# A gated graph network on one core: first states transposed by DMA in two 16-bit planes, and the first units reordered

## The chip, the cores and the metric

The kernel runs on one core of one Trainium2 chip. The metric is the device time of one execution in microseconds (us). Five engines run their own instruction streams and meet at semaphores: TensorE (PE, matmuls; PEld is its weight load), VectorE (DVE), ScalarE (ACT), GpSimd (POOL) and SyncE (SP), which here only issues DMAs. The time before is 384.85 us, the median of three runs (384.82 to 385.16).

## The reference

64 graphs of 128 nodes with 128 features. A layer norm and a ReLU give the first state h; five rounds of a gated update follow, each with its own 128x128 weight; the masked last state is added to x. All weights are float32.

```python
h = jnp.maximum(_layernorm(x, axis=-1), 0.0)
A = (adj != 0).astype(x.dtype)
for l in range(5):
    m = jnp.einsum('bnd,de->bne', h, weight[l])
    agg = jnp.einsum('bij,bid->bjd', A, m)
    gi = agg @ w_ih.T + b_ih
    gh = h @ w_hh.T + b_hh
    r = sigmoid(i_r + h_r)
    z = sigmoid(i_z + h_z)
    n = tanh(i_n + r * h_n)
    h = (1.0 - z) * n + z * h
out = x + h * nodemask[..., None]
```

## The kernel before

**Tiles and units.** Four graphs make a tile: 128 partitions by 512 columns. There are 16 tiles, in three groups (tiles 0 to 3, 4 to 9, 10 to 15). A unit is one layer of one tile, numbered K = 0 to 79: within a group all tiles do layer 0, then all do layer 1, and so on. A tile of the first group comes back every 4 units, one of the others every 6. Weight products of the input side are folded once per layer into `v_hi`/`v_lo` (`fold`, L321); `u_hi`/`u_lo` belong to the state side.

**Two layouts.** Every float32 value is split into two float16 parts, so a product is three matmuls (L250 to L252). `nat` holds a state with nodes on the partitions, for the aggregation (L308, L309: `ps_s<-a,nat`, 8 matmuls a unit). `hp` holds it with features on the partitions, for the gates (`ps_r`, `ps_z`, `ps_hn`, `ps_in`). `h` is the float32 state, features on the partitions. After a new state, ACT makes its high part, POOL its low part (L703), and a DMA transpose on SP's queue brings both from `hp` to `nat` (`transpose`, L203) for the tile's next layer.

**The first state of a tile.** DVE takes the moments (L494, L503), POOL the reciprocal root (L674, L676), DVE the shift (`shift_of`, L515), ACT the normalised values `h0` with nodes on the partitions (L375) and their high part in `nat` (L383), POOL the low part (L680). SP transposes `nat` to `hp` by DMA (`transpose_first` of SP, L197). The float32 `h` comes another way: PE transposes `h0` with four matmuls against an identity into the PSUM bank `ps_t` (L317), and ACT copies that to `h` (`transposed`, L395). For tile 0 also `hp` comes from `ps_t`.

**The order.** It is written out per engine. PE's unit K is: nine state products (`h_products`), six products of r and z with s (`s_product`), the aggregation of unit K + 1, three products for n. DVE's unit is: `r_times_hn` (L531), `n_input` (L537), `s_low` (L525) of unit K + 1, at most one preparation step, then the new state (L543, L548). The preparation of tiles 4 to 15 is spread over units by `prep` (L50 to L53): `prep[t]` is the unit of stage 0, each stage one unit later. Stage 0 moments, 1 aggregate and root, 2 shift and adjacency (POOL L686, 1.94 us each), 3 and 4 the two halves of the layer norm, 5 high and low part and PE's transposes, 6 the DMA transpose and ACT's copy to `h`. Tiles 4 to 9 have `prep` 1, 4, 7, 10, 13, 16, so that stage 2 of a tile stands in the same unit as stage 5 of the tile ahead. Within PE's loop the transposes stand ahead of the aggregation of the next unit.

**The start and the end.** Before unit 0 PE runs blank matmuls (`awake`, L325) while the inputs and weights arrive, and a power-of-two scale is taken from bounds on the weights (`weight_scale`, `scale_from_bound`). The last unit has its own code (`masked_open`, L557; `last_result`, L565).

The names above with these lines are what the change touches.

Of the kernel before, what the change touches and what calls it, by code (L numbers as in the profile page):

```python
# [32 lines left out]
def gnn_kernel(nc, x, xT, adj, mask_row, fold_lhs, w_ihT, w_hhT, bias_ih, bias_hh, ident, out):  # L33
# [35 lines left out]
    with ExitStack() as ctx:  # L69
# [42 lines left out]
        rstd = sb("rstd", [P, 2, TG])  # L112
        shift = sb("shift", [P, 2, TG])
# [5 lines left out]
        nat = ctx.enter_context(nc.sbuf_tensor("nat", [P, RING, 2 * TG, P], F16))  # L119

# [15 lines left out]
        ends_loaded = [sem(f"ends_loaded{i}") for i in range(FRING)]  # L136
        stored = [sem(f"stored{i}") for i in range(FRING)]
# [9 lines left out]
        bn_done, aggr_done, var_done, rstd_done = sem("bn_done"), sem("aggr_done"), sem("var_done"), sem("rstd_done")  # L147
        shift_done, h0_done, a_done, t_mm = sem("shift_done"), sem("h0_done"), sem("a_done"), sem("t_mm")
        nat_hi_init, nat_lo_init = sem("nat_hi_init"), sem("nat_lo_init")
        h_hi_init, h_lo_init, h_init = sem("h_hi_init"), sem("h_lo_init"), sem("h_init")  # L150
# [6 lines left out]
        last_masked, last_h_masked, last_kept, open_done, last_out, last_hn_mm = sem("last_masked"), sem("last_h_masked"), sem("last_kept"), sem("open_done"), sem("last_out"), sem("last_hn_mm")  # L157
# [27 lines left out]
        def _(sp):  # L185
# [33 lines left out]
            load_x(0)  # L219
            sp.dma_start(fold_in[:].rearrange("p (l d) -> p l d", l=L), fold_lhs).then_inc(fold_loaded, 16)  # L220
# [10 lines left out]
            for K in range(1, N + 2):  # L231
# [16 lines left out]
        def _(pe):  # L248
# [81 lines left out]
            def first():  # L330
                pe.wait_ge(blank_set, 1)
                awake(18)
# [6 lines left out]
                awake(8)  # L339
                pe.wait_ge(top_done, 1)  # L340
                pe.wait_ge(u_lo_done, 1)

            first()
            for K in range(N):
                h_products(K)
                if K == N - 1:
                    break
                if K == 0:
                    aggregate(0)
                    transpose_first(1)  # L350
# [17 lines left out]
        def _(act):  # L368
            def layernorm(t, half):
                act.wait_ge(shift_done, t + 1)  # L370
                if t >= LN:
                    act.wait_ge(nat_lo_init, t - LN + 1)
                    act.wait_ge(t_mm, t - LN + 1)
# [22 lines left out]

            def s_high(K):
# [15 lines left out]
            def gate_n(K):  # L413
                act.wait_ge(npre_done, K + 1)
                n = ps_in[K % 2] if K < N - 1 else r
                nc.scalar.activation(n[:], ps_in[K % 2][:], ACT.Tanh, bias=b_ih[:, 2:3],  # L416
# [6 lines left out]

            def v_high(l):
                act.wait_ge(v_mm, l + 1)
                nc.scalar.activation(v_hi[:, l], ps_f[:, 0:CG], ACT.Copy, scale=scale[:, 0:1]).then_inc(v_hi_done, 1)

# [5 lines left out]
            def first():  # L433
                act.dma_start(whh_sb[:], w_hhT).then_inc(whh_loaded, 16)
                act.dma_start(wih_sb[:], w_ihT).then_inc(wih_loaded, 16)

# [5 lines left out]
                act.wait_ge(whh_loaded, 16)  # L442
                act.wait_ge(scale_done, 1)
                nc.scalar.activation(u_hi[:], whh_sb[:], ACT.Copy, scale=scale[:, 0:1]).then_inc(u_hi_done, 1)
                natural_high(0)
                transposed(0)
                layernorm(1, 0)
                layernorm(1, 1)
                v_high(0)
                s_high(0)  # L450
                natural_high(1)
                if DIRECT > 1:
                    transposed_high(1)
# [3 lines left out]
            for K in range(N):  # L457
# [337 lines left out]
```

## Time and profile before

| | before |
|---|---|
| median of three runs | 384.85 us |
| profiled execution, whole | 386.38 us |
| its span | 384.4 us |
| PE busy | 367.2 us, 96% |
| DVE, ACT, POOL busy | 308.0, 295.0, 273.8 us (80%, 77%, 71%) |
| DMA transposes, hp to nat and nat to hp | 64 and 15 |
| granted TensorE clock, mean | 0.989 |

The span runs from the first to the last instruction of the profiled execution; its whole time is 1.98 us longer. A busy share is over the whole span: an engine with 80% can be at its limit in one stage and idle in another. Where instructions overlap in the pipeline, a row's duration is longer than the distance from its start to the next one's; it is the distance that an engine's order has to pay.

### The profile page before, as it was taken

How to read it: one execution, taken by the hardware profiler on the slowest of the kernel's cores; microseconds unless marked ns; L12 is line 12 of the kernel's file. 1: busy time of each engine (PE TensorE's matmuls, PEld its weight loads, DVE VectorE, ACT ScalarE, POOL GpSimd, SP SyncE). 2: the span in 40 equal slices, each digit the busy share in tenths (PEclk: the TensorE clock that was granted, in tenths of full speed). 3: DMA queues.
4: the chain of work that ended last, by engine and by line, in shares of the span. 5: the costliest groups of instructions: out<-in, count | busy, mean ns of one | idle time of the engine just before them, and what ended most of it. 6: DMA issues, size and time to landing. Idle time of an engine off the chain costs nothing.

```text
span 384.4 us, 6567 instructions
## 1 busy us (share of the span) xinstructions
PE 367.2 (96%) x2182; PEld 188.7 (49%) x2182; DVE 308.0 (80%) x568; ACT 295.0 (77%) x489; POOL 273.8 (71%) x245
## 2 busy tenths in 40 slices
PE   5867999999999999999999999999999999999992
PEld 2433555555555555555555555555545555555541
DVE  5676788888887778888888898877777778777776
ACT  3587789889978777888898977788776777677662
POOL 4456677887897678777769595947876655544796
PEclk9899999999999999999999999999999999999997
DMA  8733346396573645444366664306633342298422
GB/s 239 171 55 82 84 114 125 66 210 112 131 180 82 97 96 113 107 113 82 83 90 148 98 151 121 107 10 158 136 84 84 88 77 56 57 183 214 97 82 82
DMA packets 107793, 42.89 MB, mean 112 GB/s; under 512 B 84833, under 2 KB 101473, under 8 KB 107761
## 3 DMA queue, kind: packets, MB, share of 16 engines
q1 hardware_dynamic: 107232, 41.76, 49.5%
q10 hardware_dynamic: 432, 0.66, 0.6%
q8 instruction: 17, 0.28, 0.3%
q14 instruction: 16, 0.12, 0.1%
q0 software_dynamic: 96, 0.07, 0.1%
HBM read 17.57 MB, written 4.19 MB: 57 GB/s over the span
## 4 chain that ended last, share of the span: by engine, by line
PE 89%; DVE 4%; DMA 3%; ACT 1%; issue 1%; POOL 1%; DVEq 0%; POOLq 0%
PE ps_r L250 9%; PE ps_r L251 9%; PE ps_z L251 9%; PE ps_z L252 9%; PE ps_r L252 9%; PE ps_z L250 9%; PE ps_s L309 4%; PE ps_s L308 4%; PE ps_in L252 4%; PE ps_hn L251 4%; PE ps_in L251 4%; PE ps_hn L250 4%; PE ps_in L250 4%; PE ps_hn L252 4%; PE ps_t L317 2%; DMA hp<-nat 2%
## 5 line engine op out<-in xcount | busy, mean ns | idle before, releaser
L698 POOL TENSOR_TENSOR zh<-z,h 128x512 f32<-128x512 f32 x80 | 101.5, 1269 | 85.8 <-ACT z L411 85.4
L405 ACT ACTIVATE r<-ps_r,b_sum,unscale 128x512 f32<-128x512 f32 x80 | 62.2, 777 | 56.7 <-PE ps_r L252 54.9
L531 DVE SCALAR_TENSOR_TENSOR rhn<-ps_hn,b_hn,r 128x512 f32<-128x512 f32 x80 | 60.0, 750 | 26.2 <-ACT r L405 26.1
L703 POOL TENSOR_TENSOR hp<-h,hp 128x512 f16<-128x512 f32 x64 | 74.0, 1156 | 0.0
L537 DVE TENSOR_TENSOR ps_in<-ps_in,rhn 128x512 f32<-128x512 f32 x80 | 55.9, 699 | 19.6 <-PE ps_in L252 18.3
L416 ACT ACTIVATE ps_in<-ps_in,b_ih,unscale 128x512 f32<-128x512 f32 x79 | 59.2, 750 | 13.1 <-DVE ps_in L537 11.2
L543 DVE SCALAR_TENSOR_TENSOR ps_in<-z,ps_in 128x512 f32<-128x512 f32 x79 | 54.6, 691 | 10.4 <-ACT ps_in L416 10.4
L411 ACT ACTIVATE z<-ps_z,b_sum,unscale 128x512 f32<-128x512 f32 x80 | 61.5, 769 | 0.7 <-PE ps_z L252 0.7
L548 DVE TENSOR_TENSOR h<-zh,ps_in 128x512 f32<-128x512 f32 x78 | 53.6, 687 | 8.7 <-POOL zh L698 0.8
L525 DVE TENSOR_TENSOR s_lo<-ps_s,s_hi 128x512 f16<-128x512 f32 x80 | 54.4, 680 | 1.4 <-ACT s_hi L399 1.4
L399 ACT CAST s_hi<-ps_s 128x512 f16<-128x512 f32 x80 | 46.6, 583 | 2.6 <-PE ps_s L309 1.4
L308 PE MATMUL ps_s<-a,nat 128*128 128x128 f16 x320 | 44.3, 219 | 0.0
L309 PE MATMUL ps_s<-a,nat 128*128 128x128 f16 x320 | 44.3, 219 | 0.0
L422 ACT CAST hp<-h 128x512 f16<-128x512 f32 x64 | 40.5, 633 | 0.0
L308 PEld LDWEIGHTS ps_s<-a,nat 128*128 128x128 f16 x320 | 31.3, 98 | 8.3 <-POOL nat L680 0.6
L309 PEld LDWEIGHTS ps_s<-a,nat 128*128 128x128 f16 x320 | 31.3, 98 | 7.8
L250 PE MATMUL ps_r<-hp,u_hi 128*128 128x512 f16 x80 | 30.4, 379 | 5.0 <-DMA hp<-nat 5.0
L375 ACT ACTIVATE h<-x_in,shift,rstd 128x128 f32<-128x128 f32 x64 | 27.6, 482 | 6.9 <-DVE shift L515 6.9
L250 PE MATMUL ps_r<-s_hi,v_hi 128*128 128x512 f16 x80 | 30.3, 379 | 1.0 <-DVE s_lo L525 1.0
L250 PE MATMUL ps_z<-s_hi,v_hi 128*128 128x512 f16 x80 | 30.3, 379 | 0.0
L251 PE MATMUL ps_r<-hp,u_hi 128*128 128x512 f16 x80 | 30.3, 379 | 0.0
L252 PE MATMUL ps_r<-hp,u_lo 128*128 128x512 f16 x80 | 30.3, 379 | 0.0
(88 smaller groups left out, 745.9 us busy)
## 6 DMA issues: line engine op xcount, KB each, us to landing
x_in<-in_x SPq DMA_DIRECT2D x16, 256.0 KB, 4.6
adj_in<-in_adj SPq DMA_DIRECT2D x16, 256.0 KB, 4.1
x_out<-in_xT SPq DMA_DIRECT2D x16, 256.0 KB, 3.2
mask_in<-in_mask_row SPq DMA_DIRECT2D x16, 256.0 KB, 3.9
out<-x_out SPq DMA_DIRECT2D x15, 256.0 KB, 2.3
nat<-hp SPq DMA_TRANSPOSE x64, 3.1
fold_in<-in_fold_lhs SPq DMA_DIRECT2D x1, 320.0 KB, 4.8
out<-x_out ACTq DMA_DIRECT2D x1, 256.0 KB, 2.3
```

The lines of the kernel that those rows point to most:

```text
L250: nc.tensor.matmul(ps[:], w_hi, m_hi, start=start, stop=False)
L251: nc.tensor.matmul(ps[:], w_hi, m_lo, start=False, stop=False)
L252: return nc.tensor.matmul(ps[:], w_lo, m_hi, start=False, stop=stop)
L308: nc.tensor.matmul(block_of(ps_s, q), block_of(nat_hi(t), q), a_q, start=True, stop=False)
L309: last = nc.tensor.matmul(block_of(ps_s, q), block_of(nat_lo(t), q), a_q, start=False, stop=True)
L405: nc.scalar.activation(r[:], ps_r[:], ACT.Sigmoid, bias=b_sum[:, 0:1], scale=unscale[:, 0:1]).then_inc(r_done, 1)
L411: nc.scalar.activation(z[:, K % 2], ps_z[:], ACT.Sigmoid, bias=b_sum[:, 1:2], scale=unscale[:, 0:1]).then_inc(z_done, 1)
L416: nc.scalar.activation(n[:], ps_in[K % 2][:], ACT.Tanh, bias=b_ih[:, 2:3], scale=unscale[:, 0:1]).then_inc(n_done, 1)
L531: nc.vector.scalar_tensor_tensor(out=rhn[:], in0=ps_hn[:], scalar=b_hn[:, 0:1], in1=r[:], op0=ALU.add, op1=ALU.mult).then_inc(rhn_done, 1)
L537: nc.vector.tensor_tensor(ps_in[K % 2][:], ps_in[K % 2][:], rhn[:], ALU.add).then_inc(npre_done, 1)
L698: nc.gpsimd.tensor_tensor(zh[:, K % 2], z[:, K % 2], h[:, t % RING], ALU.mult).then_inc(zh_done, 1)
L703: nc.gpsimd.tensor_tensor(h_lo(t), h[:, t % RING], h_hi(t), ALU.subtract).then_inc(h_lo_done, 1)
```

## The change

Tiles 4 to 15 no longer use PE for `h`. At stage 6 ACT copies `h0` to `halves` as 16-bit words, all low words first and then all high words (`split`); SP transposes those 256 KB by one more DMA, right behind the `nat` to `hp` one (`transpose_halves`); at stage 8 DVE interleaves the two planes into `h` (`join`, an integer copy). The sequences of PE and ACT lose 12 groups of four transposes and 12 copies from `ps_t`. The shift is now a product on POOL, from a negated mean that DVE writes right behind the aggregate (`minus_mean`). Tiles 10 to 15 are prepared every 5 units in place of every 4.

At the start the two gate weight loads go from ACT's queue to SP's; 24 and 4 blank matmuls stand where 18 and 8 stood; unit 0's state products are ordered by which operand comes first; `natural_high(1)` stands ahead of `v_high(0)` on ACT, and the layer norm of tile 2 ahead of unit 0's gates; PE's transposes of tile 1 stand behind unit 0's products of r and z. In the last unit ACT copies the mask row to PSUM, and n stays in PSUM.

```diff
-        gap = 3 if t < starts[1] + GROUPS[1] else 4
+        gap = 3 if t < starts[1] + GROUPS[1] else 5
...
+            def transpose_halves(t):
+                sp.wait_ge(split_done, t - FIRST + 1)
+                if t - FIRST >= 2:
+                    sp.wait_ge(h_init, t - 1)
+                sp.dma_start_transpose(halves_t[:, t % 2], halves[:, t % 2].rearrange("p b c -> p (b c)")).then_inc(
+                    halves_loaded[t % 2], 16)
...
                 if K in tile_at_stage[6]:
                     transpose_first(tile_at_stage[6][K])
+                    transpose_halves(tile_at_stage[6][K])
...
-                if 2 <= K + 1 < FIRST:
+                if K + 1 < FIRST:
                     transpose_first(K + 1)
-                if K in tile_at_stage[5]:
-                    transpose_first(tile_at_stage[5][K])
...
+            def split(t):
+                act.wait_ge(h0_done, 2 * t + 2)
+                if t - FIRST >= 2:
+                    act.wait_ge(halves_loaded[t % 2], 16 * ((t - FIRST) // 2))
+                nc.scalar.copy(halves[:, t % 2], h0[:, t % LN].bitcast(U16).rearrange("p (c b) -> p b c", b=2)).then_inc(
+                    split_done, 1)
...
                 if K in tile_at_stage[6]:
-                    transposed(tile_at_stage[6][K])
+                    split(tile_at_stage[6][K])
...
+                nc.vector.tensor_scalar(minus_mean[:, t % 2], mean_var[:, t % 2, :, 0], -1.0, None,
+                                        ALU.mult).then_inc(minus_done, 1)
...
+            def join(t):
+                dve.wait_ge(halves_loaded[t % 2], 16 * ((t - FIRST) // 2 + 1))
+                if t >= RING:
+                    dve.wait_ge(masked, t - RING + 1)
+                nc.vector.tensor_copy(h[:, t % RING].bitcast(U16).rearrange("p (c b) -> p b c", b=2),
+                               halves_t[:, t % 2].rearrange("p (b g) c -> p b (g c)", b=2)).then_inc(h_init, 1)
...
-                if K in tile_at_stage[2]:
-                    shift_of(tile_at_stage[2][K])
+                if K in tile_at_stage[8]:
+                    join(tile_at_stage[8][K])
...
+                pool.wait_ge(minus_done, t + 1)
+                pool.wait_ge(rstd_done, t + 1)
+                nc.gpsimd.tensor_tensor(shift[:, t % 2], minus_mean[:, t % 2], rstd[:, t % 2], ALU.mult).then_inc(shift_done, 1)
...
-                n = ps_in[K % 2] if K < N - 1 else r
...
+                nc.scalar.copy(ps_s[:], mask_in[:, f]).then_inc(mask_moved, 1)
...
-                nc.vector.scalar_tensor_tensor(out=ps_s[:], in0=z[:, K % 2], scalar=1.0, in1=mask_in[:, f],
+                dve.wait_ge(mask_moved, 1)
+                nc.vector.scalar_tensor_tensor(out=mask_in[:, f], in0=z[:, K % 2], scalar=1.0, in1=ps_s[:],
                                                op0=ALU.subtract, op1=ALU.mult).then_inc(open_done, 1)
```

The order of ACT's first instructions, before: four layer-norm pieces (`h<-x_in,shift,rstd`) per tile, `nat<-h` the high part of `natural_high`.

```order
L387 ACTIVATE hp<-ps_t 128x512
L444 ACTIVATE u_hi<-whh_sb,scale 128x384
L383 ACTIVATE nat<-h 128x512
L395 ACTIVATE h<-ps_t 128x512
L375 ACTIVATE h<-x_in,shift,rstd 128x128 x4
L426 ACTIVATE v_hi<-ps_f,scale 128x384
L399 CAST s_hi<-ps_s 128x512
L383 ACTIVATE nat<-h 128x512
L405 ACTIVATE r<-ps_r,b_sum,unscale 128x512
```

The same stretch of ACT in the changed kernel:

```order
L416 ACTIVATE hp<-ps_t 128x512
L463 ACTIVATE u_hi<-whh_sb,scale 128x384
L412 ACTIVATE nat<-h 128x512
L404 ACTIVATE h<-x_in,shift,rstd 128x128 x4
L412 ACTIVATE nat<-h 128x512
L467 ACTIVATE v_hi<-ps_f,scale 128x384
L436 CAST s_hi<-ps_s 128x512
L424 ACTIVATE h<-ps_t 128x512
L404 ACTIVATE h<-x_in,shift,rstd 128x128 x4
L442 ACTIVATE r<-ps_r,b_sum,unscale 128x512
```

The high part of tile 1 moved ahead of `v_hi` and `s_hi`, the copy of tile 0 from `ps_t` behind them, and the layer norm of tile 2 ahead of the first `r`.

SP's queue in units 10 and 11, before (`nat<-hp` is `transpose` of the unit just done, `hp<-nat` the first transpose of tile 5):

```order
L194 DMA adj_in<-in_adj 128x4x128
L189 DMA x_in<-in_x 128x4x128
L201 DMA_TRANSPOSE hp<-nat 128x8x128
L206 DMA_TRANSPOSE nat<-hp 128x8x128
L212 DMA x_out<-in_xT 128x512
L213 DMA mask_in<-in_mask_row 128x512
```

The same place in the changed kernel:

```order
L202 DMA adj_in<-in_adj 128x4x128
L197 DMA x_in<-in_x 128x4x128
L209 DMA_TRANSPOSE hp<-nat 128x8x128
L215 DMA_TRANSPOSE halves_t<-halves 128x8x128
L221 DMA_TRANSPOSE nat<-hp 128x8x128
L227 DMA x_out<-in_xT 128x512
L228 DMA mask_in<-in_mask_row 128x512
```

One more DMA transpose stands ahead of the one that unit 10's state leaves by.

DVE in units 11 and 12, before (`shift` belongs to tile 7):

```order
L503 BN_AGGR mean_var<-bn 128x2 x4
L543 SCALAR_TENSOR_TENSOR ps_in<-z,ps_in 128x512
L548 TENSOR_TENSOR h<-zh,ps_in 128x512
L531 SCALAR_TENSOR_TENSOR rhn<-ps_hn,b_hn,r 128x512
L537 TENSOR_TENSOR ps_in<-ps_in,rhn 128x512
L525 TENSOR_TENSOR s_lo<-ps_s,s_hi 128x512
L515 SCALAR_TENSOR_TENSOR shift<-mean_var,rstd 128x4
L543 SCALAR_TENSOR_TENSOR ps_in<-z,ps_in 128x512
```

The same place in the changed kernel (`COPY h<-halves_t` is `join` of tile 5):

```order
L548 BN_AGGR mean_var<-bn 128x2 x4
L551 TENSOR_SCALAR minus_mean<-mean_var 128x4
L583 SCALAR_TENSOR_TENSOR ps_in<-z,ps_in 128x512
L588 TENSOR_TENSOR h<-zh,ps_in 128x512
L571 SCALAR_TENSOR_TENSOR rhn<-ps_hn,b_hn,r 128x512
L577 TENSOR_TENSOR ps_in<-ps_in,rhn 128x512
L565 TENSOR_TENSOR s_lo<-ps_s,s_hi 128x512
L620 COPY h<-halves_t 128x2x512
L583 SCALAR_TENSOR_TENSOR ps_in<-z,ps_in 128x512
```

The join stands where the shift stood, and a small instruction came in behind the aggregate.

## Rows read from the trace of the kernel before

**Rows 1.** Windows: us, busy PE PEld DVE ACT POOL, PEclk, DMA share, GB/s.

```profile
75.00:95.00 20.00, 20.00 (x119) 10.44 (x118) 17.57 (x38) 18.19 (x33) 15.66 (x15) 1.00 0.74 151
...
270.00:370.00 100.00, 100.00 (x602) 50.92 (x600) 79.05 (x116) 72.17 (x113) 66.27 (x56) 1.00 0.48 105
```

**Rows 2.** Waits of PE: waiting line, releaser, us in total, times, longest.

```profile
PE ps_r L250 <- DMA hp<-nat: 5.0, 3, 2.1
```

**Rows 3.** Timeline of the start, all engines: start, us, instruction.

```profile
11.93 0.58 ACT L395 ACTIVATE h<-ps_t 128x512 f32<-128x512 f32 x1
...
12.17 1.11 DVE L515 SCALAR_TENSOR_TENSOR shift<-mean_var,rstd 128x4 f32<-128x4 f32 x1
...
13.32 1.65 ACT L375 ACTIVATE h<-x_in,shift,rstd 128x128 f32<-128x128 f32 x4 [0.81 <-DVE shift L515]
...
15.17 1.01 POOL L676 TENSOR_TENSOR rstd<-var_eps,neg_half 128x4 f32<-128x4 f32 x1
...
18.05 1.16 POOL L680 TENSOR_TENSOR nat<-h,nat 128x512 f16<-128x512 f32 x1 [1.87 <-ACT nat L383]
18.08 1.41 DVE L508 TENSOR_SCALAR a<-adj_in 128x512 f16<-128x512 f32 x1
...
22.42 0.39 PE L250 MATMUL ps_r<-hp,u_hi 128*128 128x512 f16 x1 [1.57 <-DMA hp<-nat]
...
36.59 0.39 PE L250 MATMUL ps_r<-hp,u_hi 128*128 128x512 f16 x1 [1.28 <-DMA hp<-nat]
```

**Rows 4.** Window just ahead of unit 0.

```profile
11.00:14.20 3.20, 3.20 (x9) 1.21 (x8) 3.16 (x8) 2.39 (x7) 1.17 (x1) 0.52 1.21 290
```

**Rows 5.** Timeline of PE, units 8 to 10.

```profile
59.34 0.38 PE L250 MATMUL ps_r<-hp,u_hi 128*128 128x512 f16 x1
...
63.67 0.38 PE L250 MATMUL ps_r<-hp,u_hi 128*128 128x512 f16 x1
...
68.44 0.38 PE L250 MATMUL ps_r<-hp,u_hi 128*128 128x512 f16 x1
...
70.38 0.38 PE L250 MATMUL ps_r<-s_hi,v_hi 128*128 128x512 f16 x1
```

**Rows 6.** Instructions of the tiles shift, a and ps_t: ns min/median/max.

```profile
L515 DVE SCALAR_TENSOR_TENSOR shift<-mean_var,rstd x16: 148/690/1112, 7.8 to 244.0; 128x4 f32<-128x4 f32 x16
...
L508 DVE TENSOR_SCALAR a<-adj_in x4: 394/414/1405, 13.2 to 28.6; 128x512 f16<-128x512 f32 x4
...
L395 ACT ACTIVATE h<-ps_t x16: 577/586/594, 11.9 to 262.0; 128x512 f32<-128x512 f32 x16
```

**Rows 7.** Timeline of unit 9, DVE and POOL.

```profile
69.25 0.68 DVE L525 TENSOR_TENSOR s_lo<-ps_s,s_hi 128x512 f16<-128x512 f32 x1
...
69.84 0.55 DVE L515 SCALAR_TENSOR_TENSOR shift<-mean_var,rstd 128x4 f32<-128x4 f32 x1
...
70.34 1.94 POOL L686 TENSOR_SCALAR a<-adj_in 128x512 f16<-128x512 f32 x1
```

**Rows 8.** Timeline of units 10 to 13, SP, DVE, POOL and PE.

```profile
78.25 2.00 SPq L201 DMA_TRANSPOSE hp<-nat  x1
...
80.30 1.43 SPq L206 DMA_TRANSPOSE nat<-hp  x1
...
83.92 0.55 DVE L515 SCALAR_TENSOR_TENSOR shift<-mean_var,rstd 128x4 f32<-128x4 f32 x1
...
84.42 1.93 POOL L686 TENSOR_SCALAR a<-adj_in 128x512 f16<-128x512 f32 x1
...
85.75 0.22 PE L308 MATMUL ps_s<-a,nat 128*128 128x128 f16 x1
```

**Rows 9.** DMA issues between 78.2 and 81.2 us: us from issue to landing.

```profile
hp<-nat SPq DMA_TRANSPOSE x1, 4.5
nat<-hp SPq DMA_TRANSPOSE x1, 3.4
```

**Rows 10.** Timeline of the end.

```profile
378.36 1.57 DVE L562 SCALAR_TENSOR_TENSOR ps_s<-z,mask_in 128x512 f32<-128x512 f32 x1
378.48 0.78 ACT L416 ACTIVATE r<-ps_in,b_ih,unscale 128x512 f32<-128x512 f32 x1 [1.66 <-DVE ps_in L537]
```

More of the change, by code:

```diff
@@ L112, in gnn_kernel @@
         rstd = sb("rstd", [P, 2, TG])
+        minus_mean = sb("minus_mean", [P, 2, TG])
         shift = sb("shift", [P, 2, TG])
@@ L136, in gnn_kernel @@
         ends_loaded = [sem(f"ends_loaded{i}") for i in range(FRING)]
+        halves_loaded = [sem(f"halves_loaded{i}") for i in range(2)]
         stored = [sem(f"stored{i}") for i in range(FRING)]
@@ L256, in h_product, with first_h_products @@
                 return three(ps, block_of(u_hi, k), block_of(u_lo, k), h_hi(t), h_lo(t), True, k == 2)
+            def first_h_products():
+                banks = (ps_r, ps_z, ps_hn)
+                pe.wait_ge(h_hi_init, 1)
+                pe.wait_ge(u_hi_done, 1)
+                for k, ps in enumerate(banks):
+                    nc.tensor.matmul(ps[:], block_of(u_hi, k), h_hi(0), start=True, stop=False)
+                pe.wait_ge(h_lo_init, 1)
+                for k, ps in enumerate(banks):
+                    nc.tensor.matmul(ps[:], block_of(u_hi, k), h_lo(0), start=False, stop=False)
+                pe.wait_ge(u_lo_done, 1)
+                for k, ps in enumerate(banks):
+                    nc.tensor.matmul(ps[:], block_of(u_lo, k), h_hi(0), start=False, stop=k == 2)
             def h_products(K):
                 t, l = units[K]
-                if l == 0 and t < DIRECT:
-                    pe.wait_ge(h_lo_init, t + 1)
-                elif l == 0:
+                if l == 0:
                     pe.wait_ge(hp_loaded[t % RING], 16 * (t // RING + (t % RING >= DIRECT)))
@@ L338, in first @@
                 fold(0)
-                awake(8)
+                awake(4)
                 pe.wait_ge(top_done, 1)
-                pe.wait_ge(u_lo_done, 1)
             first()
             for K in range(N):
-                h_products(K)
+                if K:
+                    h_products(K)
+                else:
+                    first_h_products()
                 if K == N - 1:
@@ L414, in gate_n @@
                 act.wait_ge(npre_done, K + 1)
-                n = ps_in[K % 2] if K < N - 1 else r
-                nc.scalar.activation(n[:], ps_in[K % 2][:], ACT.Tanh, bias=b_ih[:, 2:3],
+                nc.scalar.activation(ps_in[K % 2][:], ps_in[K % 2][:], ACT.Tanh, bias=b_ih[:, 2:3],
                                      scale=unscale[:, 0:1]).then_inc(n_done, 1)
@@ L422, in state_high, with u_high @@
                 nc.scalar.copy(h_hi(t), h[:, t % RING]).then_inc(h_hi_done, 1)
+            def u_high():
+                act.wait_ge(whh_loaded, 16)
+                act.wait_ge(scale_done, 1)
+                nc.scalar.activation(u_hi[:], whh_sb[:], ACT.Copy, scale=scale[:, 0:1]).then_inc(u_hi_done, 1)
             def v_high(l):
@@ L508, in first_adjacency @@
                 nc.vector.tensor_scalar(a[:, t], adj_in[:, t], 0.0, None, ALU.not_equal).then_inc(a_done, 1)
-            def shift_of(t):
-                dve.wait_ge(rstd_done, t + 1)
-                if t >= 2:
-                    dve.wait_ge(h0_done, 2 * (t - 1))
-                nc.vector.scalar_tensor_tensor(out=shift[:, t % 2], in0=mean_var[:, t % 2, :, 0], scalar=-1.0,
-                                               in1=rstd[:, t % 2], op0=ALU.mult, op1=ALU.mult).then_inc(shift_done, 1)
             def transposed_low(t):
```

63 lines of the change are left out of this document (32 added, 31 removed).

## The prediction

> **What bounds the kernel now.** I read the windows first, then PE's waits, then the timelines of the start, of units 8 to 13 and of the end. Between 270 and 370 us PE is busy for all 100.00 us at a granted clock of 1.00, and it is just as full between 75 and 95 us, where DVE has 2.43 us of 20 idle and ACT 1.81 [rows 1]. PE waits within its unit loop three times for the first transpose of a tile, 5.0 us in all [rows 2], and the last of these ends at 36.59 us [rows 3]. So there are three stretches. Up to 36.59 us the chain through each tile's first state decides (layer norm, high part, low part, DMA transpose). From there to some 377 us it is PE's instruction count, and nothing else. At the end it is the chain of the last unit. An instruction taken from PE in the middle is worth its full length, as long as DVE, ACT, POOL and the DMAs still arrive in time; the question of this change is whether they do.
>
> **The start.** Unit 1 began at 22.42 when its transpose had landed; that was issued when POOL's low part ended at 18.05 + 1.16, and POOL had waited 1.87 us for ACT's high part [rows 3]. Its own work, the root of tile 2, ended at 15.17 + 1.01 = 16.18. In the change ACT doesn't copy `ps_t` at 11.93 but starts tile 1's layer norm there (before: 13.32, after a wait for DVE's shift, which took 1.11 us for four elements), needs 1.65 us for it and some 0.6 for the high part: ready at 14.2. So POOL's root becomes what comes last. It carries the shift as well, which I take at 0.2 us, but DVE gets to the aggregate of tile 2 up to 1.0 us earlier, without that shift. The low part starts at 15.4 to 16.4 in place of 18.05: 1.7 to 2.6 us gained for unit 1. For unit 2 the whole layer norm now lies ahead of the first gates, where half of it, 0.8 us, used to come behind n; that adds up to 0.9. For unit 3 the rest of its chain is the same, with the shift found ready. I take 3.3 us at the start of unit 3, between 2.0 and 4.2. PE's own work could hold this back: between 11.0 and 14.2 us the granted clock was 0.52 [rows 4], the lower level of 1.2 GHz, after PE had stood idle with short breaks of work. If the first unit falls into such a stretch, its nine state products take twice as long, some 1.9 us more; that delays s, and I expect it to cost the sum 1 us of the 3.3, not all, since POOL's chain doesn't pass through it. Moving the weight loads behind the first x on SP adds two issues ahead of fold and tile 1, a shift of 1 us that I cost at nothing: the order of the bytes that the weight bound needs is still x, weights, fold.
>
> **Twelve groups of transposes leave PE.** From unit 8 to unit 9 PE needs 63.67 - 59.34 = 4.33 us, from 9 to 10, with a group of four transposes, 68.44 - 63.67 = 4.77 [rows 5]. That is 0.44 us for each group, 12 x 0.44 = 5.3 us, all in the part where PE is full. ACT loses 12 copies of 0.586 us [rows 6] and gets 12 copies of 1024 16-bit words. Nothing shows such a copy; between 0.59 (the same bytes) and 1.17 (twice the elements) I take 1.0. That is 0.4 us more once in three units of 13 us, of which ACT has 9% idle, 1.2 us: it fits, though the gate behind it can be 0.4 us late.
>
> **What DVE pays.** The join moves 1024 16-bit words from SBUF to SBUF. A copy of 512 elements takes 0.414 undisturbed [rows 6], the subtraction of 512 elements 0.68 [rows 7]: below 0.41 is excluded, twice 0.68 = 1.36 is the upper end, and I take 0.75, near the copy, whose form it has. But that copy has a maximum of 1.405, and the row with 1.41 began at 18.08 beside POOL's subtraction, which ended at 19.21 [rows 3, 6]; the copy ran its 0.4 us, roughly, behind it. The shift, 148 ns at least, has a median of 690, and in unit 9 it ends at 70.39 just as POOL goes over to the adjacency at 70.34 [rows 6, 7]. So these DVE forms wait for a running POOL instruction, and the join, in the shift's place, will wait 0.5 us too: 1.2 in place of 0.55. `minus_mean` costs between 0.15 and, if it also waits for POOL, 0.7; I take 0.4. In units 9 to 17 there are three such rounds of three units. Each adds 0.65 + 0.4 to DVE and takes 0.44 from PE's time, 1.5 us, against an idle share of 2.43/20 x 13.4 = 1.6. The margin of PE itself is small: `s_lo` ends at 69.93, and PE takes it at 70.38 [rows 5, 7], 0.45 us. It fits almost exactly; I book 0.5 us of stalls, bounds 0 and 2.5 (join 1.36 and `minus_mean` 0.7 in all three rounds, less the margin). For tiles 10 to 15 a round has five units and the join's unit has no other preparation on DVE: free. Shift on POOL: 0.2 us, twelve times, where POOL has 20% idle: free.
>
> **What the DMA queue pays.** The added transpose stands between two others on SP. In unit 10 the `hp` one was issued at 78.25 and took the queue 2.00 us, and unit 10's own went out at 80.30, behind it [rows 8]. It landed 3.4 us later [rows 9], at 83.7, and PE's aggregation of that tile came at 85.75 [rows 8]: 2.05 us of margin. The change takes 0.44 of it (one group of transposes fewer between) and puts the new issue ahead, 1.3 to 2.0 us. That leaves between +0.3 and -0.4, and up to 1.1 less if it lands after 4.5, as `hp` did [rows 9]. The same holds in units 7 and 13; later tiles come back after six units and have 8.7 us more. What waits on SP behind it are only loads for later. I book 0.3 us each, 1.0 in all, bounds 0 and 4.
>
> The Trainium skill (VectorE: DVE Perf Modes, The three transpose paths) gives 390 ns for a 128x128 bf16 transpose on TensorE and 1309 ns by DMA, and advises TensorE where PSUM will do. By that the eight blocks of the planes would take 10.5 us, an estimate from that page, and each join would come six or seven us late. The trace disagrees: eight blocks land in 3.4 to 4.5 us.
>
> **A missed boundary.** The new planes go out at 80.3 and land between 83.7 and 84.8 by the two landings. The join of tile 5 comes up where the shift did, at 83.92, or 0.44 earlier. POOL goes over to the adjacency at 84.42 [rows 8]. If the planes are there, the join slips in ahead of it; if not, it waits for the planes and then for 1.93 us of adjacency. That can happen in units 9, 12, 15 and 18. A miss costs about 1.9 us less the margin of 0.45, some 1.5. I book 0.7, half a miss.
>
> The Trainium skill (SBUF — State Buffer, SBUF: two separate sides) states it as a lock on a port pair: whichever of GpSimd and a two-port DVE instruction starts first keeps it for its whole length. By that a missed boundary costs the whole adjacency, as booked; the waits of the shift above agree with it.
>
> **The end.** The masked product started at 378.36 and took 1.57 us, to 379.93, beside POOL, while n was ready at 378.48 + 0.78 = 379.26 [rows 10]. With the mask in PSUM it has one SBUF input less and should take 0.7, to 379.06, so n decides: 0.7 us gained. The copy to PSUM fits on ACT between r and n.
>
> **Sum.** Against the profiled execution's span of 384.4: -3.3 (start) - 5.3 (transposes) - 0.7 (end) + 0.5 + 1.0 + 0.7 (DVE, queue, boundary) = -7.1, so 377.3. The span and what lies around it make 386.38, but the median of the runs, 384.85, is 0.45 above the span; the predicted median is 377.75.
>
> **Rivals.** (a) *The full gain.* No stall in the middle: the bookings of 2.2 us fall away, and a start at its bound of 4.2: 377.75 - 2.2 = 375.6, at best 374.7. For it speaks that no part of units 4 to 79 shows a PE wait today. Chance 0.22. (b) *Boundaries missed.* Join late in three or four of units 9, 12, 15, 18: 3 x 1.5 or 4 x 1.5 in place of 0.7, and the queue at 2: 377.75 + 3.8 to 6.3 = 381.5 to 384. For it: the landing of 83.7 to 84.8 against 84.42. Against: the first of the four has hardly any loads beside it, and a stall of PE moves the next join later, into its landing. Chance 0.13. (c) *Slower: a slow interleave.* The write skips every second 16-bit word. If the join takes more than the upper end of the rows, it costs all 12 tiles. DVE's chain in a unit leaves 1.2 us between `s_lo` and the new state before PE stalls, so with a join of J the stall is 12 x (J + 0.2 - 1.2), and the gain of 9.3 is gone at J = 1.8. At J = 2.2 it would be 14.4: 384.85 - 9.3 + 14.4 = 390. No row shows a DVE instruction with more than 1.36 us per 1024 elements undisturbed. Chance 0.03. (d) *The reorder brings nothing*, because the loads or the clock take it back: start 0.5 in place of 3.3: 380.6. Chance 0.07.
>
> My forecast has 0.55. The range holds it with (a) nearly whole, (d) and the near part of (b): 375.0 to 381.8. Two tenths of a percent, 0.8 us, is about what a measurement of this kernel can tell. Faster holds for the forecast, (a), (d) and most of (b): 0.95; slower for (c) and the far end of (b), 0.03; the same 0.02.
>
> **What would show it.** PE's first matmul of unit 3 near 33.3 us. Units of 4.33 us without exception from unit 18 on. The join near 0.75 us at its shortest and 1.2 in the middle. PE waits in units 10 to 18 of some 2 us, on `s_lo` or on `nat`, and none later. DVE's last three instructions without a gap behind n. Wrong would be: PE waits above 4 us after unit 3, a join above 1.4 us alone, or a first unit 3 later than 35 us.

## The result, and the profile after

The changed kernel takes 383.44 us (median of seven runs, 381.68 to 383.97) against 384.82 (seven runs, 384.72 to 386.43): a ratio of 0.9946, interval 0.9927 to 0.9964. It is faster, by 0.5% in place of the 1.8% of the forecast, and outside the forecast's range. Its profiled execution took 383.44 us, with a span of 381.6: PE 96% busy, DVE 83%, ACT 78%, POOL 74%.

To see where the time went I use one measure throughout: the distance from PE's first matmul of a unit to that of the next. It is 4.33 us for a unit that waits for nothing, 4.77 with a group of four transposes [rows 5]. What a unit has over 4.33 is its stall (four units of the first group also hold a fold of 0.65 us, in every kernel here; unit 78 has 0.70 over in all of them, which is left out). Every stretch of the two profiles, predicted and measured, in us:

| | predicted | measured |
|---|---|---|
| start of unit 3 | 3.3 earlier | 2.7 earlier (36.59 to 33.91) |
| twelve groups of transposes | -5.3 | -5.3 |
| stalls, units 3 to 77 | +2.2 | +5.6, in 21 units |
| end of the span after unit 79 starts | -0.7 | -0.4 (10.73 to 10.30) |
| span | 384.4 to 377.3 | 384.4 to 381.6 |
| from span to median | +0.45 | +1.84 |

The 36.59 us and the last row belong together: the first profile of the kernel before was of a long execution. In its second profile, below, unit 3 starts at 35.26, so that the start gained 1.35 us and not 2.7; what the first row shows too much comes back in the last.

Windows of the changed kernel, columns as in [rows 1]:

```profile
75.00:95.00 20.00, 19.73 (x113) 9.35 (x111) 18.53 (x39) 18.17 (x33) 17.47 (x18) 1.00 0.86 180
270.00:370.00 100.00, 100.00 (x606) 50.94 (x604) 79.47 (x118) 72.14 (x114) 66.60 (x56) 1.00 0.47 106
```

The late stretch is unchanged. Between 75 and 95 us DVE has 1.5 us idle in place of 2.4, POOL 2.5 in place of 4.3. The waits of PE and of its weight loads, and DVE's for the planes (columns as in [rows 2]):

```profile
PEld ps_r L268 <- DVE s_lo L565: 11.7, 21, 1.9
...
PE ps_r L268 <- DMA hp<-nat: 3.0, 2, 2.1
PE ps_r L268 <- DVE s_lo L565: 2.8, 4, 1.7
...
PEld ps_s L338 <- DMA nat<-hp: 1.6, 3, 0.6
DVE h L620 <- DMA halves_t<-halves: 1.2, 3, 0.5
```

Against [rows 2], 5.0 us of waiting for a tile's first transpose have become 3.0, and a new wait for `s_lo` is there: 21 times. (A weight load that waits costs less than its wait, since it normally runs ahead.)

The start, timeline (all engines), answering to [rows 3]:

```profile
11.34 0.20 POOL L719 TENSOR_TENSOR shift<-minus_mean,rstd 128x4 f32<-128x4 f32 x1
11.80 1.64 ACT L404 ACTIVATE h<-x_in,shift,rstd 128x128 f32<-128x128 f32 x4
...
13.47 0.63 ACT L412 ACTIVATE nat<-h 128x512 f16<-128x512 f32 x1
...
15.21 0.20 POOL L719 TENSOR_TENSOR shift<-minus_mean,rstd 128x4 f32<-128x4 f32 x1
15.36 1.16 POOL L723 TENSOR_TENSOR nat<-h,nat 128x512 f16<-128x512 f32 x1
...
19.73 0.39 PE L268 MATMUL ps_r<-hp,u_hi 128*128 128x512 f16 x1 [0.86 <-DMA hp<-nat]
...
26.80 0.39 PE L268 MATMUL ps_r<-hp,u_hi 128*128 128x512 f16 x1 [2.12 <-DMA hp<-nat]
```

ACT's layer norm of tile 1 starts at 11.80 (predicted 11.93), the high part is ready at 14.10 (14.2), POOL's low part starts at 15.36 (15.4 to 16.4), and the shift on POOL takes its 0.2 us. The chain of tile 1 went as worked out. But behind the 2.12 us wait the clock fell (windows of the changed kernel):

```profile
26.00:28.00 2.00, 1.20 (x5) 0.54 (x6) 1.90 (x8) 1.97 (x5) 0.00 (x0) 0.85 0.04 6
28.00:30.00 2.00, 2.00 (x6) 0.68 (x5) 0.50 (x1) 0.53 (x2) 1.88 (x2) 0.50 0.00 0
30.00:32.00 2.00, 2.00 (x10) 1.00 (x9) 0.00 (x0) 0.72 (x2) 0.39 (x1) 0.80 0.75 141
```

0.50 is the lower level of 1.2 GHz. Unit 3 came at 33.91, 7.11 us after unit 2.

In the middle, the tile of the planes (ns min/median/max):

```profile
L215 SPq DMA_TRANSPOSE halves_t<-halves x12: 1231/1356/2507, 63.4 to 264.6; - x12
L620 DVE COPY h<-halves_t x12: 746/1366/1843, 66.8 to 267.9; 128x1024 uint16<-128x1024 uint16 x12
its engine sat idle before it (us, times) until:
  DMA halves_t<-halves: 1.2, 3
...
DMA to landing us min/median/max: 3.1/3.4/4.2
```

The join needs 0.746 us at its shortest, as I took it, but 1.37 in the median and 1.84 at most. One of the costliest, timeline of DVE, POOL and PE, in unit 24 and the two behind it:

```profile
135.49 1.26 POOL L757 TENSOR_TENSOR x_out<-x_out,mask_in 128x512 f32<-128x512 f32 x1
135.75 1.60 DVE L620 COPY h<-halves_t 128x1024 uint16<-128x1024 uint16 x1
...
136.71 1.75 POOL L741 TENSOR_TENSOR zh<-z,h 128x512 f32<-128x512 f32 x1
...
138.49 0.69 DVE L588 TENSOR_TENSOR h<-zh,ps_in 128x512 f32<-128x512 f32 x1 [0.55 <-POOL zh L741]
...
140.55 0.68 DVE L565 TENSOR_TENSOR s_lo<-ps_s,s_hi 128x512 f16<-128x512 f32 x1
...
141.29 0.39 PE L268 MATMUL ps_r<-s_hi,v_hi 128*128 128x512 f16 x1 [0.57 <-DVE s_lo L565]
```

The join is issued 0.26 us after a POOL product starts and does most of its 0.75 us of work behind that product's end (136.75). It ends at 137.35, 0.60 us behind that end; in this profile 11 of the 12 joins end 0.59 to 0.61 us behind the POOL instruction with two SBUF inputs that was running when they were issued. Then POOL's next product, `zh`, takes 1.75 in place of 1.27, because the join runs. DVE waits 0.55 for `zh`, and everything behind moves: `s_lo` is late, PE stands still. A join thus costs twice, once by its own wait and once by the delay that it passes on. Not all of this stall is the join's: unit 26 has 0.96 us here, and 0.34 in the run below in which PE does the transposes again.

The end, DVE's and ACT's part, answering to [rows 10]:

```profile
375.99 0.68 DVE L603 SCALAR_TENSOR_TENSOR mask_in<-z,ps_s 128x512 f32<-128x512 f32 x1
376.12 0.75 ACT L452 ACTIVATE ps_in<-ps_in,b_ih,unscale 128x512 f32<-128x512 f32 x1 [1.17 <-DVE ps_in L577]
376.90 0.70 DVE L611 TENSOR_TENSOR ps_in<-mask_in,ps_in 128x512 f32<-128x512 f32 x1 [0.23 <-ACT ps_in L452]
377.63 0.69 DVE L614 TENSOR_TENSOR x_out<-x_out,ps_in 128x512 f32<-128x512 f32 x1
```

The masked product takes 0.68 in place of 1.57 and n decides, as predicted. Counted from the start of unit 79, DVE's last instruction ends 0.8 us earlier than before; but the store behind it landed after 2.6 us and not after 2.3, and the span gained 0.4.

### The profile page after: what moved, and what is told of

Read it like the earlier page. It is cut to its first block, busy times and chain, and to the rows that moved or that the text cites. A ratio compares the mean times of both kernels' runs of the same rounds, so it can differ in the third digit from the quotient of the medians.

```text
span 381.6 us, 6527 instructions
## 1 busy us (share of the span) xinstructions
PE 366.9 (96%) x2136; PEld 181.8 (48%) x2136; DVE 317.8 (83%) x580; ACT 298.9 (78%) x490; POOL 280.8 (74%) x261
## 4 chain that ended last, share of the span: by engine, by line
PE 70%; DVE 13%; POOL 4%; DMA 3%; issue 3%; ACT 3%; SPq 2%; DVEq 0%; POOLq 0%; ACTq 0%
PE ps_r L268 7%; PE ps_z L269 7%; PE ps_z L268 7%; PE ps_z L270 7%; PE ps_r L269 7%; PE ps_r L270 7%; PE ps_s L339 4%; PE ps_s L338 4%; PE ps_in L270 4%; PE ps_in L269 4%; PE ps_in L268 4%; PE ps_hn L269 3%; PE ps_hn L270 3%; PE ps_hn L268 3%; DVE ps_in L577 2%
## 5 line engine op out<-in xcount | busy, mean ns | idle before, releaser
L741 POOL TENSOR_TENSOR zh<-z,h 128x512 f32<-128x512 f32 x80 | 102.7, 1284 | 79.5 <-ACT z L448 79.2
L452 ACT ACTIVATE ps_in<-ps_in,b_ih,unscale 128x512 f32<-128x512 f32 x80 | 60.1, 751 | 21.6 <-DVE ps_in L577 20.1
L268 PE MATMUL ps_r<-hp,u_hi 128*128 128x512 f16 x79 | 30.0, 379 | 3.4 <-DMA hp<-nat 3.0
L269 PE MATMUL ps_r<-s_lo,v_hi 128*128 128x512 f16 x80 | 30.5, 381 | 0.0
L270 PE MATMUL ps_r<-s_hi,v_lo 128*128 128x512 f16 x80 | 30.3, 379 | 0.0
```

What stands on the lines that cost most here:

```text
L268: nc.tensor.matmul(ps[:], w_hi, m_hi, start=start, stop=False)
L269: nc.tensor.matmul(ps[:], w_hi, m_lo, start=False, stop=False)
L270: return nc.tensor.matmul(ps[:], w_lo, m_hi, start=False, stop=stop)
L452: nc.scalar.activation(ps_in[K % 2][:], ps_in[K % 2][:], ACT.Tanh, bias=b_ih[:, 2:3], scale=unscale[:, 0:1]).then_inc(n_done, 1)
L741: nc.gpsimd.tensor_tensor(zh[:, K % 2], z[:, K % 2], h[:, t % RING], ALU.mult).then_inc(zh_done, 1)
```

## The experiments

Each was timed against the kernel before, whose median was 384.8 to 384.9 in every comparison.

**The kernel before, once more** (no edit).

> The kernel before, unchanged, for a second profile. Its first profile took 386.38 us while its runs have a median of 384.8, so 1.5 us of that span are not usual. Theory: they lie ahead of unit 3 (first matmul of unit 3 near 35.1 us in place of 36.59), and then the reordered start gained 1.2 us in the median and not the 2.7 us that the two profiles show. Rival: unit 3 starts at 36.6 again, and the 1.5 us lie elsewhere.

385.06 us, span 383.1. From its timeline:

```profile
16.66 1.16 POOL L680 TENSOR_TENSOR nat<-h,nat 128x512 f16<-128x512 f32 x1 [0.33 <-ACT nat L383]
...
21.03 0.39 PE L250 MATMUL ps_r<-hp,u_hi 128*128 128x512 f16 x1 [1.57 <-DMA hp<-nat]
...
35.26 0.39 PE L250 MATMUL ps_r<-hp,u_hi 128*128 128x512 f16 x1
```

There the clock was 1.00 from 10 to 28 us, unit 3 started at 35.26 and not at 36.59, and all behind it took the same time. So the profile of [rows 3, 4] was that of a long execution (386.38 us against a median of 384.85). What differs between the two is the stretch at 0.52: there the first matmul of unit 0 came at 14.27, here at 12.73, and ACT's high part of tile 1, which stands behind the `s_hi` of unit 0, followed it. POOL waits 0.33 us for that high part here, and 1.87 in [rows 3]. The usual start of POOL's low part, against which the changed kernel's 15.36 has to be held, is 16.66 and not 18.05.

The 0.45 of my sum is no error of its own, since the forecast is the median before less 7.1 us whatever the span. The error lies in the start, which I read from the long execution. In every profiled execution from here on the time is 1.8 to 2.0 us above the span.

**Transposes back on PE; start, end, shift on POOL and the gap of 5 kept.**

```diff
-                    split(tile_at_stage[6][K])
+                    transposed(tile_at_stage[6][K])
...
-                    transpose_halves(tile_at_stage[6][K])
...
-                    join(tile_at_stage[8][K])
...
+                    transpose_first(tile_at_stage[5][K])
```

> The changed kernel with the transposes of tiles 4 to 15 back on PE and ACT's copy from ps_t; no split, no third DMA, no join; start, end, shift on POOL and the gap of 5 stay. Theory (the joins' stalls eat what the transposes free): the middle has 5.3 us of transposes again and nearly no waits, so 383.4 +- 0.6 us, as the changed kernel. Rival (2 us or more of the stalls come from the negated mean on DVE and the shift on POOL): these waits stay, 385 us or more.

382.38 us, ratio 0.9942 (0.9928 to 0.9956): within the intervals the same as the whole change, and 0.4 below the range that I expected. What gained is the start and the end; the DMA transposes with their joins bring nothing net. The twelve units with transposes take 4.77 each, so the 5.3 us are real and are all given back. Unit 3 starts at 32.44 here, without a stretch at the lower clock: the start is worth 2.8 us against 35.26. Two stalls of 0.34 and 0.20 in units 26 and 29 are there without any join.

**The planes are made and moved, but the interleave isn't done.** `h` of tiles 4 to 15 gets zeros (512 columns for tiles 4 to 9, one for 10 to 15).

```diff
-                nc.vector.tensor_copy(h[:, t % RING].bitcast(U16)...
+                columns = TILE if t < GROUPS[0] + GROUPS[1] else 1
+                nc.vector.memset(h[:, t % RING, 0:columns], 0.0).then_inc(h_init, 1)
```

> The changed kernel with the interleave left out: tiles 4 to 9 get a plain DVE memset of the same 512 float32 columns, tiles 10 to 15 a memset of one column, so the state of these tiles is wrong and only the time counts. Split and the third DMA stay. Theory (DVE's join on the shared port is what PE waits for): the waits of units 30 to 56 vanish (1.9 us) and those before shrink to what DMA and ACT leave: 379.5 to 380.5. Rival (SP's queue and ACT's split): not under 382.5.

379.65 us (378.17 to 380.33), ratio 0.9856 (0.9839 to 0.9874). With split, DMA and queue all kept, the median is 3.8 us below the changed kernel's. The profiled execution is the fastest of its four: unit 3 starts at 32.01, the clock holds, and its stalls add up to 2.1 us, those of the changed kernel to 5.6. The difference of 3.5 is what the join costs beyond the memset in its place, which takes 0.48 us for each of tiles 4 to 9 and 0.06 for the others; it is one profile against one. One stall of 0.60 (unit 16, `nat` late) is the queue's.

**Tiles 4 to 9 by PE, 10 to 15 by DMA.**

```diff
+HALF = 10
...
-                    split(tile_at_stage[6][K])
+                    (split if tile_at_stage[6][K] >= HALF else transposed)(tile_at_stage[6][K])
...
-                if K in tile_at_stage[8]:
+                if tile_at_stage[8].get(K, 0) >= HALF:
```

> Tiles 4 to 9 transposed by PE as before, tiles 10 to 15 by DMA in two planes. Theory: PE has 2.6 us more of transposes, and the waits of units 10 to 26 (3.5 us) are nearly gone, those of units 30 to 56 (1.9 us) stay: 382.5, range 381.8 to 383.3. Rival (waits in units 10 to 26 come from the shift and the negated mean): 385.

381.32 us, ratio 0.9915 (0.9899 to 0.9931), 0.5 below the range expected. So even half of the change is better than the whole. The joins of tiles 10 to 15, which I had called free, leave stalls of 0.13, 0.22, 0.21, 0.21 and 0.48 us in units 31, 36, 41, 46 and 51, 1.25 in all, for 2.6 us of transposes removed.

**The changed kernel, once more** (no edit).

> The changed kernel again, beside the others. In its first profile TensorE's granted clock was 0.50 from 28 to 30 us, in unit 2, after PE had waited 2.1 us for a transpose; unit 3 began at 33.91. In the three profiles with the same start that had no such stretch it began at 32.0 to 32.5. Theory (a clock stretch of 1.5 us comes in some executions): runs fall into two clusters about 1.5 us apart, near 381.8 and 383.4. Rival (the spread has another cause): a profile with unit 3 near 32.5 still takes 383.4.

383.15 us (381.72 to 384.44), ratio 0.9957 (0.9939 to 0.9974). The clock fell in the same place (0.50 between 28 and 30 us), unit 3 at 34.08. The two clusters of runs did not come: the six lie at 381.72, 382.62, 383.00, 383.29, 384.01 and 384.44. The stalls added up to 6.1 us in the profiled execution: units 15 and 17 had 0.49 and 0.62 where the first profile had 0.31 and 0.30. Ahead of unit 17 one join missed its place: the planes of tile 6 came 0.35 us late, and the adjacency had begun 0.08 us before the join (DVE and POOL):

```profile
95.78 1.94 POOL L729 TENSOR_SCALAR a<-adj_in 128x512 f16<-128x512 f32 x1
95.86 1.13 DVE L620 COPY h<-halves_t 128x1024 uint16<-128x1024 uint16 x1 [0.35 <-DMA halves_t<-halves]
```

The join took 1.13 us. It did not wait for the adjacency's end at 97.72.

**Transposes on PE, and tiles 10 to 15 every 4 units again.**

```diff
-        gap = 3 if t < starts[1] + GROUPS[1] else 5
+        gap = 3 if t < starts[1] + GROUPS[1] else 4
```

> The transposes of tiles 4 to 15 on PE and the gap of 4 again: only the start, the end, the shift on POOL and the negated mean remain of the change. With the gap of 5 PE stalled 0.34 us in unit 26 and 0.20 in unit 29 beyond its transposes. Theory (the gap of 5 puts the adjacency of tile 10 into unit 23, where POOL already has the final of tile 2): both stalls go, 0.5 us less, 381.8. Rival (they come from the shift on POOL): unchanged, 382.4.

382.97 us, ratio 0.9948 (0.9933 to 0.9964); the 0.5 us less than the run before it can't be seen in the times. In the profile the stall of 0.34 in unit 26 is gone, so the gap of 5 made it: it puts tile 10's adjacency into unit 23, beside POOL's results of finished tiles. The one in unit 29 (0.23) stays. Three runs are at 381.9 to 382.3 and three at 383.6 to 383.7, with mean clocks of 0.996 to 0.998 and 0.992 to 0.993. The distance is about the 1.5 us that the stretch at 0.50 costs in the start, but no profile of a slower one shows where its time went.

**Tiles 10 to 15 by DMA, with the join behind the new state and not ahead of it** (the edit against the kernel with tiles 4 to 9 by PE).

```diff
-                if tile_at_stage[8].get(K, 0) >= HALF:
-                    join(tile_at_stage[8][K])
...
+                if tile_at_stage[8].get(K, 0) >= HALF:
+                    join(tile_at_stage[8][K])
                 if K == N - 2:
                     masked_state(K)
```

> Tiles 10 to 15 by DMA, tiles 4 to 9 by PE, as in the run before it, but the join stands behind the new state of its unit, when POOL has nothing to do. Theory (what hurts is the wait for a running POOL instruction, 1.57 us in place of 0.75): the join takes 0.75, the waits of units 31 to 56 (1.25 us) go, 380.1. Rival (the DVE time itself hurts, or the delayed POOL instruction): no gain or a loss, 381.3 or more.

379.93 us (379.35 to 380.14), ratio 0.9870 (0.9857 to 0.9882). The join's row in this kernel (ns min/median/max):

```profile
L624 DVE COPY h<-halves_t x6: 741/746/1074, 158.1 to 266.4; 128x1024 uint16<-128x1024 uint16 x6
```

And one of them in the timeline of POOL and DVE:

```profile
177.82 1.16 POOL L750 TENSOR_TENSOR hp<-h,hp 128x512 f16<-128x512 f32 x1
...
179.73 0.74 DVE L624 COPY h<-halves_t 128x1024 uint16<-128x1024 uint16 x1
...
180.92 1.27 POOL L745 TENSOR_TENSOR zh<-z,h 128x512 f32<-128x512 f32 x1 [1.94 <-ACT z L452]
```

In the changed kernel the join of this tile was issued at 180.10 with POOL's low part running from 179.91, and took 1.57. One place further down DVE's order, POOL stands idle and waits for z. The five stalls of 1.25 us are gone.

**All joins behind the new state** (tiles 4 to 8 one unit later), the negated mean on POOL, tile 10 one unit later.

```diff
+    joining = {prep[t] + (9 if t < 9 else 8): t for t in prep}
+    prep[10] += 1
...
+                nc.gpsimd.tensor_tensor(minus_mean[:, t % 2], mean_var[:, t % 2, :, 0], minus_one[:], ALU.mult).then_inc(minus_done, 1)
```

> All of tiles 4 to 15 by DMA, the join behind the new state (tiles 4 to 8 one unit later than in the change, the others in the same unit), the negated mean on POOL in place of DVE, and the preparation of tile 10 one unit later. Theory (DVE's waits for the port and POOL's crowding in unit 23 are what the freed 5.3 us went into): the waits of PE fall from 5.7 to 1.5 us or less, 379.0, range 378.0 to 380.5. Rival (SP's queue and ACT's longer copy are as dear as the port): 382 or more.

381.08 us (380.52 to 382.45), ratio 0.9910 (0.9896 to 0.9923): 2.4 us better than the changed kernel, 2.1 worse than expected. About 1 us of that lies in the start: the clock was 0.81 and 0.53 between 14 and 20 us, unit 3 starts at 33.82 where the late join of tiles 10 to 15 alone had 32.88, and the mean clock of all six runs is 0.986 to 0.992. The median join is at 0.74 here too, but a stall of 0.86 us is left in unit 26:

```profile
133.77 1.27 POOL L758 TENSOR_TENSOR x_out<-x_out,mask_in 128x512 f32<-128x512 f32 x1
...
135.00 1.27 POOL L742 TENSOR_TENSOR zh<-z,h 128x512 f32<-128x512 f32 x1
...
136.30 0.69 DVE L588 TENSOR_TENSOR h<-zh,ps_in 128x512 f32<-128x512 f32 x1 [1.09 <-POOL zh L742]
136.90 1.08 DVE L620 COPY h<-halves_t 128x1024 uint16<-128x1024 uint16 x1
...
137.88 0.73 DVE L571 SCALAR_TENSOR_TENSOR rhn<-ps_hn,b_hn,r 128x512 f32<-128x512 f32 x1
...
140.06 0.39 PE L271 MATMUL ps_r<-s_hi,v_hi 128*128 128x512 f16 x1 [0.57 <-DVE s_lo L565]
```

Two things add up. POOL's own order is full around unit 24, which delays `zh` and the new state without any join. And tile 9's join, now behind that late state, takes 1.08 beside POOL's low part and stands ahead of `rhn` and `s_lo`. The run before this one has no join there: its new state came no earlier (136.53), `rhn` followed at once, and its stall in unit 26 is 0.33. So a place behind the new state is free only while DVE has time there. Unit 13 has 0.71, 0.5 of it a wait for `nat`.

**The changed kernel with 14 more blank matmuls** (6 ahead of the first product of s, 8 behind unit 1), to keep PE busy in the start.

```diff
+                    awake(6)
...
+                if K == 1:
+                    awake(8, ps_f)
```

> The changed kernel with 14 more blank matmuls: 6 ahead of unit 0's products with s and 8 ahead of unit 2, where PE otherwise waits 1.7 and 2.1 us. Theory (the spread of 381.7 to 384.4 us is a stretch at half clock after one of these waits): no granted clock under 1.00 between 14 and 36 us, unit 3 near 32.5, the runs close together, median 381.8. Rival (the spread comes from the middle): the clock is full, but the runs still spread over 2 us.

384.44 us (twelve runs, 382.74 to 384.76), ratio 0.9976 (0.9964 to 0.9988). The clock was 1.00 all through the start, and unit 3 came 0.7 us earlier, at 33.17. Yet the kernel is slower than the changed one and its runs still spread over 2 us, as the rival said; my theory that the spread of the runs is the clock's alone fell. The stalls come to 7.6 us, and 2.07 of them are in unit 20. The tile of the planes between 104 and 112 us:

```profile
L623 DVE COPY h<-halves_t x1: 854/854/854, 110.7 to 110.7; 128x1024 uint16<-128x1024 uint16 x1
its engine sat idle before it (us, times) until:
  DMA halves_t<-halves: 2.2, 1
...
DMA to landing us min/median/max: 5.3/5.3/5.3
```

Issued at 105.39, like the changed kernel's at 105.41, these planes landed after 5.3 us and not after 3.5. The join had to wait 2.20 us in DVE's order, and PE lost 2.07. That is the late join of rival (b) in one tile; which transfer delayed the planes stays open.

**Tiles 10 to 15 by DMA with the late join, and other units for their preparation**: 26, 30, 35, 39, 42 and 46, away from POOL's full units; then the same with the blank matmuls.

```diff
+    prep.update({10: 26, 11: 30, 12: 35, 13: 39, 14: 42, 15: 46})
```

> As the hybrid with the late join, and tiles 10 to 15 prepared from units 26, 30, 35, 39, 42, 46, so that tile 10's adjacency stays clear of the finals of tiles 0 to 3 and no join meets a moments step. Theory: the waits of units 26 and 29 (0.55 us) go, nothing new comes: 379.4. Rival (a shorter gap makes new waits at units 43 to 47): 380 or more.

> e10 with the 14 blank matmuls. If e10's runs hold executions with the slow stretch, these are gone: 379.3, spread under 0.5 us. Where e10 had none, no difference beyond 0.2 us.

381.17 us (ratio 0.9902, 0.9879 to 0.9925) and 380.68 (0.9890, 0.9872 to 0.9909). The stall in unit 26 is gone, but new ones in units 45 to 54 add up to 1.2 us: moving the crowd made another. Both miss the 379.4 and 379.3 expected, and the second spreads over 1.9 us and not 0.5. The clock was 1.00 through the start in both profiles, so what the blank matmuls did to it can't be seen here; the times agree within the intervals. Both are no better than the late join alone.

**All tiles by DMA, all joins late, that plan, the negated mean of tiles 4 to 15 on POOL, the blank matmuls.**

> All of tiles 4 to 15 by DMA, joins behind the new state, the negated mean of tiles 4 to 15 on POOL, the preparation plan of e10, and the blank matmuls. Middle: 2.6 us of transposes fewer than e11, against waits of units 9 to 24 which were 1.9 us in the kernel with all joins late. Theory: 378.6, range 377.9 to 379.5, the fastest. Rival (SP's queue is the next limit and gives it all back): 379.5 or more.

379.85 us (379.27 to 381.20), ratio 0.9872 (0.9852 to 0.9893). Stalls 2.5 us in place of 5.6, unit 3 at 32.79. The 378.6 expected did not come; the median lies where the rival, a queue that gives the gain back, put it. In the profile 0.66 of the stalls is unit 10, where `nat` landed late, and 0.43 each are units 51 and 54. Together with the late join of tiles 10 to 15 alone (379.93) it is the fastest complete version, 1.3% below the kernel before; the two can't be told apart. So no gain from taking tiles 4 to 9 off PE, too, can be measured here; the other preparation plan, with its stalls in units 51 and 54, is part of that.

## Why the prediction was wrong

Two steps failed: what DVE pays, and the size of the start. The forecast was the median before less 7.1 us, and the change gained 1.4. The 5.7 us between them are 3.4 of stalls, 1.95 of start and 0.3 of end. The stalls alone would have left the time inside the range (377.75 + 3.4 = 381.15).

**The start** was mis-sized: 3.3 us booked, 1.35 gained (35.26 to 33.91). Its chain came as worked out for tile 1, with POOL's low part at 15.36. But I held it against the 18.05 of a long execution, in which POOL's wait of 1.87 us for ACT came with the slow clock; against the usual 16.66, unit 1 gained 1.3 us and not 1.7 to 2.6. The 0.9 booked for tile 2 was there in the chain, POOL's low part coming 2.25 us earlier (21.02 for 23.27), but tile 2's transpose then landed after 4.5 us in place of 3.6, and unit 2 gained 1.3 like unit 1. What slowed that landing is open. Unit 3 gained 1.35 in the profile in which the clock fell behind the 2.12 us wait, and 2.1 to 3.3 where the clock held. I had placed the fall of the clock ahead of unit 0, by [rows 4]; it came in unit 2, where the kernel before lost next to nothing by it: in its second profile the clock was 0.50 between 30 and 32 us too, but unit 3 came 7.14 us after unit 2, against 7.08 in [rows 3], where 1.28 of them are a wait for its transpose. The changed kernel has no such wait left in front of unit 3, and there the slow stretch shows.

**The transposes** were right: 12 times 0.44, all in the full stretch. `split` took 1.03 us, predicted 1.0.

**What DVE pays is the step that failed most.** I booked 0.5 us for DVE and 0.7 for missed boundaries; the join costs 3.5, by the profile of the kernel without the interleave. (The negated mean adds some 0.2, in unit 29, see below.) Its own work was right (0.746 for 0.75). Three things were wrong. The wait for POOL: 1.2 us in all was read from the shift, which needs 0.15 itself and stood at one lucky place in POOL's order; the join is in the median at 1.37. The delay passed on to `zh` was not in the sum at all. And "for tiles 10 to 15: free" counted idle DVE time over a round of five units, where a stall comes from one chain in one unit: the slack of 0.45 us between `s_lo` and PE [rows 5, 7] was the number to hold the join's 1.57 against. These five stalls are 1.25 us, and they go when the join moves one place.

**The missed boundary** happened in no unit of the changed kernel's first profile: the joins of tiles 4 to 6 slipped in ahead of the adjacency. In its second profile tile 6 missed it, and the join took 1.13 us and not 0.75 + 1.93; unit 17 has 0.3 more than in the first. So the price of 1.5 us was wrong. What costs more is planes that land late; with the blank matmuls it was 2.07 us in one unit.

**The queue** cost about 0.6 us: one late `nat`, as foreseen, though in unit 16, 13 or 10 by the kernel; the 1.0 booked holds it. The gap of 5 cost 0.34, which I hadn't priced.

**The end**: 0.4 of 0.7 us; the chain gained its part, and the last store landed later.

**The rivals.** (a) asked for no stall in the middle; with all tiles by DMA even the best version keeps 2.5 us. (b) gives the right number, 381.5 to 384, but by another mechanism: joins that collide with POOL's two-input instructions, not joins that miss the adjacency, and with a start that gained less. (c) fell: 0.746 us shows no slow interleave. (d) fell: the reorder is the part that brought the gain.

**The stall of 0.2 us in unit 29** is there with and without joins, in all ten profiles in which DVE writes tile 10's negated mean; that instruction takes 1.15 to 1.19 us there, beside a running POOL instruction. It is absent in the two in which POOL writes it. That is the likely cause, though no run changed this alone.

**Open**: what makes the planes, and tile 2's transpose, land late at times; and how the spread of 2 to 3 us within the runs of one kernel divides into clock and stalls.

## What to carry to other kernels

Moving work from the bounding engine to a nearly full one must be priced at the place where it lands: the slack of that unit's chain, and what the neighbouring engine is doing just then, not the idle share of a stretch. When an added instruction costs more than its work, first look at which instruction of the neighbouring engine it overlaps; here one place in an engine's order was worth 1.4 us, about as much as the whole change. And compare a profiled execution's own time with the median before reading a gain from its rows: here 1.4 us of the start belonged to that one execution.

## What the runs showed of the hardware

**DVE and POOL exclude each other, but not in every order.** The join (SBUF to SBUF) took 0.74 to 0.75 us beside an idle POOL. When a POOL instruction with two SBUF tensors was already running, it ended some 0.60 us behind that one's end, and took up to 1.84 in all. Started first, it made POOL wait: `zh` 1.75 for 1.27, the adjacency (one input) 2.40 for 1.94. But with the adjacency already running, no join waited for its end (DVE and POOL, kernel with blank matmuls):

```profile
66.63 1.94 POOL L732 TENSOR_SCALAR a<-adj_in 128x512 f16<-128x512 f32 x1
67.23 0.74 DVE L623 COPY h<-halves_t 128x1024 uint16<-128x1024 uint16 x1 [1.05 <-DMA halves_t<-halves]
```

In the same kernel at 110.32 and 110.68 it took 0.85, and in the changed kernel's second profile, shown above, 1.13. The Trainium skill (SBUF — State Buffer, SBUF: two separate sides) says that whichever starts first holds the pair of ports that the two share for its whole length. The joins beside two-input instructions agree; these three, behind an adjacency that had started, do not, and the 1.9 us of waiting by which I priced a missed boundary were not paid in any of them.

**Small instructions pay the same wait.** `minus_mean` works on four elements: 0.17 us alone, 0.59 in the median, 1.18 beside `zh`.

**The clock.** After PE's wait of 2.12 us the granted clock was 0.85, 0.50 and 0.80 in the stretches shown above. Kernels with the same start kept 1.00 there without a blank matmul (unit 3 at 32.0 to 32.9), so it is not shown that blank matmuls are what holds it. From unit 2 to unit 3 the changed kernel took 7.11 us, these took 5.55 to 5.96: the stretch cost 1.15 to 1.56 us where nothing else was waiting.

**DMA transposes.** The planes, 256 KB from SBUF to SBUF, landed in 3.1 to 5.3 us, and their issue held the queue for 1.23 to 2.51 us.
